# The causal mask of a transformer layer's attention, moved from a matmul in front of the scores to an addition in PSUM behind them

## The chip, the cores and the metric

One NeuronCore of a Trainium2 chip runs the whole kernel; nothing is exchanged with another core. The metric is the device time of one execution in microseconds. The engines that matter here are TensorE (matmuls, written PE in the profile; its weight loads PEld), VectorE (DVE), ScalarE (ACT), GpSimd (POOL) and the DMA queues. Each engine takes its instructions in program order and is kept in step with the others by semaphores.

## What is computed

A pre-norm transformer layer on x of 2 sequences x 1024 positions x 256: attention with 16 heads of 128, then a routed mixture of 32 experts with 8 chosen per token, and two shared blocks.

```python
k = jnp.einsum('ihd,bpd->biph', W_K, x)
q = jnp.einsum('ihd,bpd->biph', W_Q, x)
v = jnp.einsum('ihd,bpd->biph', W_V, x)
scores = jnp.einsum('biph,biqh->biqp', k, q)
mask = jnp.tril(jnp.ones((pos, pos), dtype=x.dtype))
masked = scores * mask - jnp.float32(10000000000.0) * (1.0 - mask)
attn = jax.nn.softmax(masked / jnp.sqrt(jnp.float32(d_head)), axis=-1)
z = jnp.einsum('biqp,biph->biqh', attn, v)
out = jnp.einsum('df,bqf->bqd', W_O, z_flat)
...
x = x + attention(layernorm(x))
x = x + experts(layernorm(x))
```

## The kernel before

**Pairs of heads.** The attention runs over 16 pairs of heads: 8 pairs of sequence 0 (numbered 0 to 7 here), then 8 of sequence 1 (8 to 15). Every product is made as three fp32r matmuls of a high and a low part (`three`, L780 to L784), so each result in PSUM is taken twice: ScalarE copies the high part, VectorE subtracts it from PSUM for the low part.

**Rows of scores.** A head has eight rows of scores, r = 0 to 7; row r is 128 queries by the first 128(r+1) keys. `scores` (L820) writes it into one of two PSUM tiles ps_s of 1024 columns. Its first matmul, L827, is the mask: a bf16 matmul of `causal` (0 on and below the diagonal, -1e30 above) with an identity `ident_bf` into the diagonal 128 columns, with the products then added onto it. VectorE takes the negated maximum of the row (`maximum`, L1310, the reduction at L1312), ScalarE the exponential with the sum of the row (`exponentials`, L1113, at L1116) into `prob`. The tile is free for row r+2 after the exponential.

**What follows a row.** TensorE transposes blocks of prob into one of two banks ps_t (`transpose`, L836, at L841); ScalarE copies the high part pT_hi (L1132) and VectorE makes pT_lo (L1327; pL_hi and pL_lo for the last block of a half); then TensorE multiplies with v into ps_z, VectorE and ScalarE split z (L1334, L1135), and TensorE projects the output into ps_t (two results of 128x256), which VectorE adds to `acc` (L1342). Between these run the projections of the next heads' q, k and v through the bank ps_x, each with its ScalarE copy (L1105, L1107, L1110) and VectorE subtraction (L1298, L1302, L1307).

**The order.** It is written out by hand in tables of items that TensorE, ScalarE and VectorE all walk, each taking its own part of every item. `T` is a transposition, `R` a row of scores, `X` a projection of q, k or v, `V` a product with v, `W` an output projection; the first number is the half (0 to 3: two heads, two halves of 512 queries each). The steady pairs (0 to 6 and 11 to 14, in two loops) use this one:

```python
PAIR = """
T0.0 R0.0 R0.1 T0.1 T0.2 X0 R0.2 R0.3 V0.0 T0.3 X1 V0.1 V0.2 T1.0 T1.1 V0.3 X2 R1.0 R1.1 W0.0
W0.1 X3 V1.0 T1.2 T1.3 R1.2 V1.1 V1.2 V1.3 T1.4 T1.5 X4 V1.4 T1.6 T1.7 R1.3 V1.5 X5 V1.6 V1.7 T2.0
T2.1 R2.0 R2.1 W1.0 X6 T2.2 R2.2 R2.3 W1.1 V2.0 T2.3 X7 V2.1 V2.2 T3.0 T3.1 V2.3 X8 T3.2 R3.0 R3.1
W2.0 X9 W2.1 V3.0 T3.3 V3.1 T3.4 V3.2 T3.5 V3.3 V3.4 T3.6 T3.7 R3.2 V3.5 V3.6 V3.7 X10 R3.3 W3.0 W3.1 X11
"""
```

The rows of a half are made while the half before is worked off: R0.0 to R0.3 are needed whole by T1.0, R1.0 to R1.3 by T2.0, R2.0 to R2.3 by T3.0, R3.0 to R3.3 by the next pair's T0.0. R0.* and R2.* are the wide rows 4 to 7, R1.* and R3.* the rows 0 to 3. Pair 7 (MIDDLE) and pair 8 (ROUTE) have the layer norms and the router's logits woven in, pairs 9 and 10 the routing tables, pair 15 (LAST) has no next pair's rows and ends in the experts. START, in front of pair 0, makes the first four rows and the first projections. Behind the attention (from about 991 us) come the experts, which use ps_s, ps_t and ps_z in other ways.

**Set-up.** GpSimd builds `ident`, `ident_bf`, `causal` and others at the start and counts them on `s_const`; TensorE waits for 8 of them.

Of the kernel before, what the change touches and what calls it, by code (L numbers as in the profile page):

```python
# [12 lines left out]
P = 128  # L13
# [266 lines left out]
def width(r):  # L280

    return P * (r + 1)
# [7 lines left out]
def build(nc, ctx, x, w_a, w_b, w_o, router, bias, experts, out):  # L290
# [12 lines left out]
    xT_lo = sb("xT_lo", [P, ND, B * S], F32R)  # L303
    ident, ident_bf = sb("ident", [P, P]), sb("ident_bf", [P, P], BF16)
    causal = sb("causal", [P, P], BF16)
# [117 lines left out]
    s_pool = sem("pool_hi")  # L423
    s_scores, s_max, s_exp = sem("scores"), sem("max"), sem("exp")
    s_bank, s_hi, s_bank_free = sem("bank"), sem("pT_hi"), sem("bank_free")
# [24 lines left out]
    WS0, YS0 = 16, 16  # L450
    CONSTS = 25 + WORD

# [122 lines left out]
    def _(pool):  # L575
        pool.memset(ident[:, :], 0.0).then_inc(s_const, 1)
        pool.memset(neg_half[:, :], -0.5).then_inc(s_const, 1)
        pool.memset(zero[:, :], 0.0).then_inc(s_const, 1)
        pool.memset(ident_bf[:, :], 0.0).then_inc(s_const, 1)
        pool.memset(causal[:, :], 0.0).then_inc(s_const, 1)  # L580
        pool.wait_ge(s_const, 5)
        for m in (ident, ident_bf):
            pool.affine_select(out=m[:, :], in_=m[:, :], compare_op=ALU.not_equal, fill=1.0,
                               base=0, pattern=[[-1, P]], channel_multiplier=1).then_inc(s_const, 1)
        pool.affine_select(out=causal[:, :], in_=causal[:, :], compare_op=ALU.is_ge, fill=MASKED,
# [60 lines left out]
        pool.iota(thr_int, pattern=[[P, NT]], base=0, channel_multiplier=0).then_inc(s_const, 1)  # L646
        pool.wait_ge(s_const, 18 + 1 + WORD)
        pool.tensor_copy(number[:, :], number_int).then_inc(s_const, 1)
# [127 lines left out]
    def _(pe):  # L776
        pe.sem_inc(s_pv, PV0)
        pe.wait_ge(s_const, 8)

        def three(to, w_hi, w_lo, m_hi, m_lo, start, stop, joins=False):  # L780

            pe.matmul(to, w_hi, m_hi, start=start, stop=False, skip_group_check=joins)  # L782
            pe.matmul(to, w_hi, m_lo, start=False, stop=False, skip_group_check=joins)  # L783
            return pe.matmul(to, w_lo, m_hi, start=False, stop=stop, skip_group_check=joins)  # L784

# [34 lines left out]
        def scores(a, r, row, x_need):  # L820


            pe.wait_ge(s_exp, row + EXP0 - 1)
            pe.wait_ge(s_x_free, x_need + X0)
            q = slice(r * P, (r + 1) * P)
            to = ps_s[r % 2]
            pe.matmul(to[:, r * P:(r + 1) * P], ident_bf[:, :], causal[:, :], start=True, stop=False,  # L827
                      skip_group_check=True)
            for k0 in range(0, width(r), NQ):
                k1 = max(min(width(r), k0 + NQ), k0 + 2 * P)  # L830
                diagonal = k0 <= r * P < k1
                last = three(to[:, k0:k1], q_hi[a][:, q], q_lo[a][:, q], k_hi[a][:, k0:k1],
                             k_lo[a][:, k0:k1], not diagonal, True, diagonal)
            last.then_inc(s_scores, 1)
# [409 lines left out]
    def _(dve):  # L1244
# [65 lines left out]
        def maximum(r, row):  # L1310
            dve.wait_ge(s_scores, row + 1)
            dve.tensor_reduce(neg_max[:, r:r + 1], ps_s[r % 2][:, 0:width(r)], AX.X, ALU.max,  # L1312
                              negate=True).then_inc(s_max, 1)
# [235 lines left out]
        for kind, k, n, m in walk(START):  # L1549
            bank = [ps_x, ps_z][(m or 0) % 2]  # L1550
            if kind == "N":
                norm(k, n)
            elif kind == "Y":
                xn_low(k, n, bank, m)
            elif kind == "X":
                project(k, bank, m)
            elif kind == "R":
                maximum(n, n)
        dve.wait_ge(s_in, 32)
# [105 lines left out]
```

## Time and profile before

| | us |
|---|---|
| time, median of 3 runs | 1381.85 |
| lowest and highest run | 1377.54, 1383.18 |
| profiled execution: its span, first to last instruction | 1405.0 |
| PE busy | 1328.9 (95%) |
| PEld busy | 1171.3 (83%) |
| DVE busy | 905.6 (64%) |
| ACT busy | 722.3 (51%) |
| POOL busy | 571.1 (41%) |

The profiled execution is one execution, 1.7% above the median of the timed ones; no time of it other than its span is given. Rows of the trace are times within it, from its first instruction on. PE's matmuls are pipelined, so their busy times overlap and the distance from one start to the next is what an instruction takes. A bracket at the end of a timeline's row gives the idle time of that engine in front of the row, and the instruction that ended it. Idle time is given only where an engine waited, and a busy sum counts overlap once.

### The profile page before, as it was taken

Reading aid. Unit: us, or ns where it says so; the run is one execution under the profiler, and the core shown is the slowest. Engines: PE = TensorE matmul, PEld = TensorE weight load, DVE = VectorE, ACT = ScalarE, POOL = GpSimd, SP = SyncE. Lnnn points to the kernel's source line nnn. Section 1 sums busy time; section 2 is a strip of 40 time slices with the busy share of each in tenths; the row PEclk is TensorE's granted clock in tenths of the full one; section 3 lists DMA queues with packets and bytes.
Section 4 is the critical chain, followed back from the end, with each engine's and each line's share of the span. In section 5 each row is a group of like instructions: output and inputs, shape, how many; then the busy total and the mean of one; then the engine's idle time right before and its main releaser. Section 6 shows DMA issues by size and latency. Waiting matters only on the chain.

```text
span 1405.0 us, 28535 instructions
## 1 busy us (share of the span) xinstructions
PE 1328.9 (95%) x8578; PEld 1171.3 (83%) x8578; DVE 905.6 (64%) x1875; ACT 722.3 (51%) x1688; POOL 571.1 (41%) x587
## 2 busy tenths in 40 slices
PE   5999999999999899999999999999889997989998
PEld 4888888888888787888778888888779887978886
DVE  5667666666667878687886666666776632345536
ACT  2655555555555555554445555555455553545443
POOL 5535535355232223213043635441003664546554
PEclk9999999999999999999999999999999998999999
DMA  3253544525533000000001201020459996899963
GB/s 118 83 173 105 188 164 133 172 97 183 164 135 102 19 20 16 16 16 20 12 31 60 66 27 68 34 86 0 151 202 311 368 337 237 307 363 378 302 200 116
DMA packets 128246, 195.98 MB, mean 139 GB/s; under 512 B 10400, under 2 KB 99744, under 8 KB 128160
## 3 DMA queue, kind: packets, MB, share of 16 engines
q1 hardware_dynamic: 64752, 110.04, 23.4%
q10 hardware_dynamic: 51120, 51.26, 10.9%
q0 software_dynamic: 12288, 33.57, 6.8%
q8 instruction: 50, 0.82, 0.2%
q14 instruction: 36, 0.29, 0.1%
HBM read 107.79 MB, written 87.03 MB: 139 GB/s over the span
## 4 chain that ended last, share of the span: by engine, by line
PE 82%; DVE 7%; issue 3%; ACT 3%; DMA 3%; another core or an unknown queue 1%; SPq 1%; ACTq 0%; POOL 0%; POOLq 0%; DVEq 0%
PE ps_s L782 9%; PE ps_t L841 8%; PE ps_s L784 8%; PE ps_s L783 8%; PE ps_x L782 6%; PE ps_x L783 6%; PE ps_x L784 6%; PE ps_z L782 5%; PE ps_z L784 5%; PE ps_z L783 5%; PE ps_t L1006 3%; PE ps_z L1006 3%; PE ps_s L975 2%; PE ps_t L782 2%; PE ps_t L783 2%
## 5 line engine op out<-in xcount | busy, mean ns | idle before, releaser
L1116 ACT ACTIVATE prob<-ps_s,neg_max 128x128 f32<-128x128 f32 (+7 forms) x256 | 189.4, 741 | 256.3 <-DVE neg_max L1312 252.1
L1327 DVE TENSOR_TENSOR pT_lo<-ps_t,pT_hi 128x512 fp32r<-128x512 f32 (+2 forms) x320 | 189.4, 603 | 104.9 <-ACT pT_hi L1132 101.3
L1132 ACT ACTIVATE pT_hi<-ps_t 128x512 fp32r<-128x512 f32 (+2 forms) x320 | 161.4, 533 | 94.8 <-PE ps_t L841 92.1
L1312 DVE TENSOR_REDUCE neg_max<-ps_s 128x1 f32<-128x128 f32 (+7 forms) x256 | 186.8, 748 | 14.0 <-PE ps_s L784 11.5
L679 POOL DMA_INDIRECT xs<-xn,slots x128 | 127.7, 997 | 134.8 <-PE ps_z L1006 67.6
L841 PE MATMUL ps_t<-ident,prob 128*128 128x128 f32 x1152 | 170.8, 274 | 9.4 <-ACT prob L1116 4.2
L841 PEld LDWEIGHTS ps_t<-ident,prob 128*128 128x128 f32 x1152 | 136.7, 140 | 33.1 <-DVE pT_lo L1327 5.7
L782 PE MATMUL ps_s<-k_hi,q_hi 128*128 128x512 f32 (+2 forms) x384 | 154.7, 403 | 0.0
L1524 DVE TENSOR_TENSOR h<-sg,ps_s 128x256 f32<-128x256 f32 x112 | 46.9, 418 | 155.9 <-ACT sg L1166 103.9
L782 PE MATMUL ps_s<-ring,a_hi 128*128 x384 | 125.5, 327 | 14.3 <-SPq L530 11.9
L784 PE MATMUL ps_s<-k_hi,q_lo 128*128 128x512 f32 (+2 forms) x384 | 133.7, 348 | 0.0
L783 PE MATMUL ps_s<-k_lo,q_hi 128*128 128x512 f32 (+2 forms) x384 | 132.7, 346 | 0.0
L594 POOL TENSOR_TENSOR a_hi<-raw_a,zero 128x512 fp32r<-128x512 f32 x32 | 33.3, 1041 | 243.3 <-PE ps_x L784 158.3
L782 PE MATMUL ps_z<-pT_hi,v_hi 128*128 128x512 f32 (+2 forms) x320 | 121.8, 381 | 0.5 <-DVE pT_lo L1327 0.5
L784 PE MATMUL ps_z<-pT_hi,v_lo 128*128 128x512 f32 (+2 forms) x320 | 115.5, 361 | 0.0
L783 PE MATMUL ps_z<-pT_lo,v_hi 128*128 128x512 f32 (+2 forms) x320 | 115.4, 361 | 0.0
L1166 ACT ACTIVATE sg<-ps_s 128x256 f32<-128x256 f32 x112 | 43.5, 388 | 139.3 <-PE ps_s L784 82.2
L783 PE MATMUL ps_s<-ring,a_hi 128*128 x384 | 109.9, 286 | 0.1
L784 PE MATMUL ps_s<-ring,a_lo 128*128 x384 | 109.5, 285 | 0.0
L1342 DVE SCALAR_TENSOR_TENSOR acc<-ps_t,inv_sum,acc 128x256 f32<-128x256 f32 x256 | 108.2, 474 | 0.2 <-PE ps_t L784 0.2
L782 PEld LDWEIGHTS ps_s<-ring,a_hi 128*128 128x128 f32 x384 | 74.3, 194 | 24.3 <-issue 22.0
L594 POOL TENSOR_TENSOR o_hi<-raw_o,zero 128x256 fp32r<-128x256 f32 x32 | 20.7, 647 | 168.1 <-PE ps_z L784 167.8
(306 smaller groups left out, 3682.9 us busy)
## 6 DMA issues: line engine op xcount, KB each, us to landing
ring<-ws SPq DMA_DIRECT2D x56, 512.0 KB
xs<-taken SPq DMA_DIRECT2D x16, 1536.0 KB, 9.8
xq<-xs ACTq DMA_DIRECT2D x48, 512.0 KB
xs<-yq ACTq DMA_DIRECT2D x48, 512.0 KB
ws<-split_to SPq DMA_DIRECT2D x34, 512.0 KB, 3.1
raw<-experts_dram SPq DMA_DIRECT2D x34, 256.0 KB, 3.4
raw_a<-w_a_dram SPq DMA_DIRECT2D x15, 512.0 KB, 4.4
ring_down<-experts_dram SPq DMA_DIRECT2D x56, 128.0 KB
```

What stands on the lines that cost most here:

```text
L594: pool.tensor_tensor(hi, src, zero[:, 0:1].to_broadcast([P, src.shape[-1]]), ALU.add).then_inc(s_pool, 1)
L679: pool.indirect_dma_start(xs[b], bass.IndirectOffsetOnAxis(ap=slots[b][:, t, k:k + 1], axis=0), xn[:, t, :], None).then_inc(s_xs[b], 16)
L782: pe.matmul(to, w_hi, m_hi, start=start, stop=False, skip_group_check=joins)
L783: pe.matmul(to, w_hi, m_lo, start=False, stop=False, skip_group_check=joins)
L784: return pe.matmul(to, w_lo, m_hi, start=False, stop=stop, skip_group_check=joins)
L841: last = pe.transpose(bank[:, j * P:(j + 1) * P], prob[c][:, j, n * P:(n + 1) * P], ident[:, :])
L1006: last = pe.matmul(to, hT[g % 2][:, at], downs[g][j], start=what == "m" or j == 0, stop=what == "m" or j == 1)
L1116: act.activation(prob[c][:, j, 0:width(r)], ps_s[r % 2][:, 0:width(r)], ACT.Exp, bias=neg_max[:, r:r + 1], accum_out=row_sum[:, c, j:j + 1 ...
L1132: act.activation(to, ps_t[m % 2][:, j * P:], ACT.Copy).then_inc(s_hi, 1)
L1312: dve.tensor_reduce(neg_max[:, r:r + 1], ps_s[r % 2][:, 0:width(r)], AX.X, ALU.max, negate=True).then_inc(s_max, 1)
L1327: dve.tensor_tensor(lo, ps_t[m % 2][:, j * P:], hi.bitcast(F32), ALU.subtract).then_inc(s_bank_free, 1)
L1342: last = dve.scalar_tensor_tensor(to, ps_t[m % 2][:, j * D:(j + 1) * D], inv_sum[:, c, q:q + 1], to, ALU.mult, ALU.add)
```

## The change

The mask matmul of every row is gone, and with it `ident_bf` and its two set-up instructions on GpSimd. Every group of a row's matmuls now starts afresh. `maximum` first adds `causal` to the diagonal block of the row in PSUM, in place, with a semaphore `s_masked` of its own, and the reduction waits for that. At the first row VectorE also waits for the constants. The tables of items are not touched. The counts of `s_const` are two lower.

```diff
@@ scores, on TensorE
             q = slice(r * P, (r + 1) * P)
             to = ps_s[r % 2]
-            pe.matmul(to[:, r * P:(r + 1) * P], ident_bf[:, :], causal[:, :], start=True, stop=False,
-                      skip_group_check=True)
             for k0 in range(0, width(r), NQ):
                 k1 = max(min(width(r), k0 + NQ), k0 + 2 * P)
-                diagonal = k0 <= r * P < k1
                 last = three(to[:, k0:k1], q_hi[a][:, q], q_lo[a][:, q], k_hi[a][:, k0:k1],
-                             k_lo[a][:, k0:k1], not diagonal, True, diagonal)
+                             k_lo[a][:, k0:k1], True, True)
             last.then_inc(s_scores, 1)
@@ on VectorE
         def maximum(r, row):
             dve.wait_ge(s_scores, row + 1)
+            block = ps_s[r % 2][:, r * P:width(r)]
+            dve.tensor_tensor(block, block, causal[:, :], ALU.add).then_inc(s_masked, 1)
+            dve.wait_ge(s_masked, row + 1)
             dve.tensor_reduce(neg_max[:, r:r + 1], ps_s[r % 2][:, 0:width(r)], AX.X, ALU.max,
                               negate=True).then_inc(s_max, 1)
...
             elif kind == "R":
+                if n == 0:
+                    dve.wait_ge(s_const, MASKS)
                 maximum(n, n)
@@ on GpSimd, set-up
-        pool.memset(ident_bf[:, :], 0.0).then_inc(s_const, 1)
...
-        for m in (ident, ident_bf):
-            pool.affine_select(out=m[:, :], in_=m[:, :], compare_op=ALU.not_equal, fill=1.0,
-                               base=0, pattern=[[-1, P]], channel_multiplier=1).then_inc(s_const, 1)
+        pool.affine_select(out=ident[:, :], in_=ident[:, :], compare_op=ALU.not_equal, fill=1.0,
+                           base=0, pattern=[[-1, P]], channel_multiplier=1).then_inc(s_const, 1)
```

In program order VectorE has, at the head of the steady pair (from the transposition T0.0 to the row R0.3), before:

```order
L1327 TENSOR_TENSOR pT_lo<-ps_t,pT_hi 128x512
L1331 RECIPROCAL inv_sum<-row_sum 128x4
L1311 ISA
L1312 TENSOR_REDUCE neg_max<-ps_s 128x1
L1311 REGISTER_ALU
L1312 TENSOR_REDUCE neg_max<-ps_s 128x1
...
L1302 SCALAR_TENSOR_TENSOR q_lo<-ps_x,q_hi 128x512
L1311 REGISTER_ALU
L1312 TENSOR_REDUCE neg_max<-ps_s 128x1
```

The same place in the changed kernel, from its second subtraction on:

```order
L1326 TENSOR_TENSOR pT_lo<-ps_t,pT_hi 128x384
L1325 REGISTER_ALU
L1326 TENSOR_TENSOR pT_lo<-ps_t,pT_hi 128x256
L1290 ISA
L1298 SCALAR_TENSOR_TENSOR q_lo<-ps_x,q_hi 128x512
L1307 REGISTER_ALU
L1309 TENSOR_TENSOR ps_s<-ps_s,causal 128x128
L1311 TENSOR_REDUCE neg_max<-ps_s 128x1
```

Every reduction has an addition in front of it, and nothing else has moved: in all VectorE's program has 1168 rows where it had 1032.

## Rows read from the trace of the kernel before

**Rows 1.** Windows: us, then each engine's busy us (and instructions), PEclk, DMA share, GB/s
```profile
213.10:272.10 59.00, 59.00 (x379) 52.00 (x378) 39.53 (x76) 32.56 (x76) 27.67 (x24) 1.00 0.46 151
449.00:516.90 67.90, 63.91 (x394) 55.80 (x392) 52.92 (x106) 35.01 (x80) 17.44 (x22) 0.95 0.05 17
516.90:585.20 68.30, 65.31 (x414) 55.55 (x413) 52.47 (x109) 36.02 (x83) 17.45 (x22) 1.00 0.06 17
585.20:648.60 63.40, 60.89 (x381) 52.43 (x380) 49.84 (x132) 32.35 (x77) 13.93 (x12) 1.00 0.06 18
648.60:716.50 67.90, 61.97 (x381) 52.35 (x379) 58.02 (x112) 32.64 (x79) 16.00 (x14) 1.00 0.05 16
776.30:836.10 59.80, 59.36 (x379) 52.08 (x378) 39.59 (x76) 32.34 (x76) 29.28 (x28) 1.00 0.16 53
```

**Rows 2.** Source L827, TensorE: duration ns min/median/max, first and last start
```profile
L827 PE MATMUL ps_s<-causal,ident_bf x256: 216/229/314, 26.2 to 988.4; 128*128 128x128 bf16 x128
```

**Rows 3.** Timeline of TensorE, pair 3, row R0.3: start, us, instruction
```profile
219.19 0.23 PE L827 MATMUL ps_s<-causal,ident_bf 128*128 128x128 bf16 x1
...
219.54 0.39 PE L783 MATMUL ps_s<-k_lo,q_hi 128*128 128x512 f32 x1
219.77 0.39 PE L784 MATMUL ps_s<-k_hi,q_lo 128*128 128x512 f32 x1
```

**Rows 4.** VectorE: two groups by shape (busy, mean ns), then two dependent instructions in order of time
```profile
L1327 DVE TENSOR_TENSOR pT_lo<-ps_t,pT_hi 128x256 fp32r<-128x256 f32 x64 | 26.8, 418 | 16.0 <-ACT pT_hi L1132 14.7
L1327 DVE TENSOR_TENSOR pL_lo<-ps_t,pL_hi 128x128 fp32r<-128x128 f32 x64 | 18.3, 286 | 30.1 <-ACT pL_hi L1132 30.1
...
714.25 0.24 DVE L1499 TENSOR_TENSOR gain<-gain,bit 1x95 f32<-1x95 f32 x1
714.53 0.24 DVE L1501 TENSOR_REDUCE bits<-gain 1x6 f32<-1x96 f32 x1
```

**Rows 5.** Timeline of VectorE, pair 3, head
```profile
215.21 1.85 DVE L1312 TENSOR_REDUCE neg_max<-ps_s 128x1 f32<-128x640 f32 x2
218.49 0.89 DVE L1327 TENSOR_TENSOR pT_lo<-ps_t,pT_hi 128x384 fp32r<-128x384 f32 x2 [1.44 <-ACT pT_hi L1132]
219.30 0.68 DVE L1302 SCALAR_TENSOR_TENSOR q_lo<-ps_x,q_hi 128x512 fp32r<-128x512 f32 x1
219.90 2.22 DVE L1312 TENSOR_REDUCE neg_max<-ps_s 128x1 f32<-128x896 f32 x2
```

**Rows 6.** Timeline of ScalarE, pair 3, head
```profile
217.09 0.90 ACT L1116 ACTIVATE prob<-ps_s,neg_max 128x768 f32<-128x768 f32 x1 [0.17 <-DVE neg_max L1312]
...
221.01 1.01 ACT L1116 ACTIVATE prob<-ps_s,neg_max 128x896 f32<-128x896 f32 x1 [1.79 <-DVE neg_max L1312]
...
222.15 1.12 ACT L1116 ACTIVATE prob<-ps_s,neg_max 128x1024 f32<-128x1024 f32 x1
```

**Rows 7.** Timeline of TensorE, pair 3: the transposes T1.0 and T1.1
```profile
223.78 1.04 PE L841 MATMUL ps_t<-ident,prob 128*128 128x128 f32 x8
```

**Rows 8.** Timeline of ScalarE and TensorE, pair 10: the last wide row and T3.0
```profile
691.95 1.12 ACT L1116 ACTIVATE prob<-ps_s,neg_max 128x1024 f32<-128x1024 f32 x1 [1.17 <-DVE neg_max L1312]
...
693.30 0.96 PE L841 MATMUL ps_t<-ident,prob 128*128 128x128 f32 x7 [0.33 <-ACT prob L1116]
```

**Rows 9.** Timeline of ScalarE and TensorE, pair 3: the last wide row and T3.0
```profile
250.85 1.12 ACT L1116 ACTIVATE prob<-ps_s,neg_max 128x1024 f32<-128x1024 f32 x1 [0.53 <-DVE neg_max L1312]
...
253.19 1.03 PE L841 MATMUL ps_t<-ident,prob 128*128 128x128 f32 x8
```

**Rows 10.** Timeline of VectorE, pair 12: the maximum of row R1.3
```profile
803.35 0.69 DVE L1312 TENSOR_REDUCE neg_max<-ps_s 128x1 f32<-128x512 f32 x1 [1.27 <-PE ps_s L784]
```

**Rows 11.** Timeline, pair 10: TensorE's W0.0, and VectorE without idle time around R2.3
```profile
663.84 0.35 PE L782 MATMUL ps_t<-o_hi,z_hi 128*128 128x256 f32 x1 [0.65 <-DVE pT_lo L1327]
...
690.71 1.22 DVE L1312 TENSOR_REDUCE neg_max<-ps_s 128x1 f32<-128x1024 f32 x1
```

**Rows 12.** Timeline of TensorE, pair 7: the transpose T2.0
```profile
478.31 0.66 PE L841 MATMUL ps_t<-ident,prob 128*128 128x128 f32 x4 [2.13 <-DVE pT_lo L1327]
```

More of the change, by code:

```diff
@@ L303, in build @@
     xT_lo = sb("xT_lo", [P, ND, B * S], F32R)
-    ident, ident_bf = sb("ident", [P, P]), sb("ident_bf", [P, P], BF16)
+    ident = sb("ident", [P, P])
     causal = sb("causal", [P, P], BF16)
@@ L423, in build @@
     s_pool = sem("pool_hi")
-    s_scores, s_max, s_exp = sem("scores"), sem("max"), sem("exp")
+    s_scores, s_masked, s_max, s_exp = sem("scores"), sem("masked"), sem("max"), sem("exp")
     s_bank, s_hi, s_bank_free = sem("bank"), sem("pT_hi"), sem("bank_free")
@@ L450, in build @@
     WS0, YS0 = 16, 16
-    CONSTS = 25 + WORD
+    MASKS = 6
+    CONSTS = 23 + WORD
     X_SCORES = [X0 + x_before + count_of(order, ("M", b, 0)) + 1
@@ L578, in _ @@
         pool.memset(zero[:, :], 0.0).then_inc(s_const, 1)
-        pool.memset(ident_bf[:, :], 0.0).then_inc(s_const, 1)
         pool.memset(causal[:, :], 0.0).then_inc(s_const, 1)
-        pool.wait_ge(s_const, 5)
-        for m in (ident, ident_bf):
-            pool.affine_select(out=m[:, :], in_=m[:, :], compare_op=ALU.not_equal, fill=1.0,
-                               base=0, pattern=[[-1, P]], channel_multiplier=1).then_inc(s_const, 1)
+        pool.wait_ge(s_const, 4)
+        pool.affine_select(out=ident[:, :], in_=ident[:, :], compare_op=ALU.not_equal, fill=1.0,
+                           base=0, pattern=[[-1, P]], channel_multiplier=1).then_inc(s_const, 1)
         pool.affine_select(out=causal[:, :], in_=causal[:, :], compare_op=ALU.is_ge, fill=MASKED,
@@ L646, in _ @@
         pool.iota(thr_int, pattern=[[P, NT]], base=0, channel_multiplier=0).then_inc(s_const, 1)
-        pool.wait_ge(s_const, 18 + 1 + WORD)
+        pool.wait_ge(s_const, 16 + 1 + WORD)
         pool.tensor_copy(number[:, :], number_int).then_inc(s_const, 1)
@@ L777, in _, with three @@
         pe.sem_inc(s_pv, PV0)
[L778 to L784, printed above, removed]
+        pe.wait_ge(s_const, MASKS)
+        def three(to, w_hi, w_lo, m_hi, m_lo, start, stop):
+            pe.matmul(to, w_hi, m_hi, start=start, stop=False)
+            pe.matmul(to, w_hi, m_lo, start=False, stop=False)
+            return pe.matmul(to, w_lo, m_hi, start=False, stop=stop)
         def transpose_xn(q, d, bank):
```

## The prediction

> **What bounds the kernel now.** I read the busy time by stretch first, then TensorE's and VectorE's single rows, then the timeline of one pair of heads on three engines, then the waits. In a steady pair TensorE is busy 59.00 of 59.00 us and VectorE 39.53 [rows 1]. Seven pairs (0 to 6) look like this. So in them every TensorE instruction has its price, and work on VectorE looks free. That second half is what has to be tested, because VectorE and ScalarE take their work in program order and hand each other results. Pairs 7 to 10 carry the layer norm and the routing as well: VectorE is busy 49.84 to 58.02 us of 63.4 to 68.3, and TensorE is idle 2.5 to 5.9 us in each. Pairs 11 to 14 are like pair 12: 59.8 us, TensorE idle 0.4 [rows 1]. Nothing after 991 us touches the change.
>
> **What is removed.** 256 matmuls on TensorE [rows 2]. Their busy 229 ns overlaps others, so the price is taken from starts: from the mask's start to the second ordinary matmul is 219.54 - 219.19 = 0.35 us, and an ordinary one follows the next at 219.77 - 219.54 = 0.23 [rows 3]. A mask costs 0.12 us. 16 a pair make 1.9 us, all 256 make 30.5. The Trainium skill ("TensorE: Matmul & The Clock Gate", section "Back-to-back issue gap") gives about 81 ns to a bf16 matmul of 128 columns in a stream, which would make it 20.7 us. The row decides; what the smaller price would do stands at the sum. The two set-up instructions that GpSimd loses lie in the first 3 us, where TensorE waits for the norm: nothing. Shifting the constants' count moves no wait that ends last.
>
> **What is added.** 256 VectorE additions of 128 columns, PSUM plus SBUF into PSUM, each followed by a wait of the maximum on it. The trace has no write to PSUM by VectorE. The nearest row is the subtraction of 128 columns from PSUM, 286 ns [rows 4]. Today the next instruction starts 0.08 us before its forerunner ends (219.90 against 219.30 + 0.68, [rows 5]); one that waits for its forerunner starts 0.04 us after its end (714.53 against 714.25 + 0.24, [rows 4]). A row of scores then takes VectorE e = 0.286 + 0.04 = 0.32 us more, before its maximum is out. Low end: no overlap is lost, 0.20. High end: the write to PSUM costs as much as 128 columns more, 0.42 [rows 4] + 0.03 = 0.45. I take 0.32, nearest in shape. The Trainium skill ("VectorE: DVE Perf Modes", "The DRAIN you can't avoid") says that a semaphore between two VectorE instructions costs nothing extra, as the next never starts before the pipe is empty. By it e would be 0.29, and the sum 2 us less. These rows disagree by the 0.08.
>
> **Where it falls in a steady pair.** Take the head of pair 3. VectorE reduces two rows from 215.21 on, in 1.85 us, idles 1.44 until ScalarE's copy, takes q_lo at 219.30 and two more rows from 219.90 [rows 5]. ScalarE takes the exponential of the second row at 217.09, having waited for its maximum, then the copies and q_hi, then waits 1.79 for the third row's maximum, and starts the fourth row's exponential at 222.15, which ends at 223.27 [rows 6]. So VectorE's 1.44 of idle time is no cover: it waits there for ScalarE, which waits for VectorE. Step by step: row one is late by 0.32. Row two adds another 0.32, less 0.18 because VectorE waited a little for its scores (an estimate, from the 0.17 that ScalarE idled there): 0.46. The copies, q_hi and q_lo carry 0.46. Rows three and four are back to back: 0.78 and 1.10. TensorE begins the transposes that need row four at 223.78 [rows 7], 0.51 after 223.27. The least distance is seen where it does wait: 693.30 - 693.07 = 0.23 [rows 8]. So 0.28 is slack, and 1.10 - 0.28 = 0.82 us is a new wait on TensorE. The k part of the next projection comes out of the same chain and makes it 0.87. The four masks saved in front of it buy nothing: TensorE only arrives earlier at a later event.
>
> The other twelve masks are worth 12 x 0.12 = 1.43. Against them: the second head chain (rows R2.0 to R2.3) makes its last exponential late by 1.0 us, where TensorE has 253.19 - 251.97 = 1.22 of distance [rows 9], less 0.23 needed and less the masks saved: it gives back 0.14; and the small waits at the output projections and the last products, where a buffer is freed just in time, give back 0.14. Pair: +0.87 - 1.43 + 0.28 = -0.28 us. Seven pairs: **-2.0**.
>
> **Pairs 11 to 14.** VectorE's maximum at 803.35 starts 1.27 us late for no reason that the row shows, [rows 10], and TensorE, whose next transposes need its exponential, is idle 0.44 in the pair [rows 1]. There e adds at once, and what follows on VectorE is late too: I take +0.2 a pair, **+0.8**.
>
> **Pairs 7 to 10.** VectorE is nearly full and TensorE already waits behind it. In pair 10 the waits at 663.84 (0.65) and 693.30 (0.33) stand behind stretches in which VectorE has hardly any idle time (its reduction at 690.71 starts with none in front) [rows 8, 11], so a row of scores in such a stretch costs its 0.32, and the mask saved there nothing. Reading the stretches, I count 11 of 16 rows on the path in pair 10 (+3.6), 7 in pairs 9 and 8 each (+2.3 and +2.1), and 3 in pair 7 after its saved masks (+1.0): **+9.0**. Were all 64 rows on the path it would be +20.5; were none, -7.7.
>
> **Ends.** The last pair's twelve rows partly end in front of the experts: **+1.5**; the four rows of the start: **+0.2**.
>
> **Sum.** -2.0 + 0.8 + 9.0 + 1.5 + 0.2 = +9.5 us: 1414.5 against the profiled 1405.0, which is 1.7% over the median of the runs shown. Carried over to that median, 1381.85 + 9.5 = 1391.4. With e = 0.20 (0.12 less), some 3.7 rows a pair on the chain make seven pairs 3.2 us shorter, pairs 11 to 14 1.0, the 28 rows counted in pairs 7 to 10 3.4 and the ends 0.4: +1.5, 1383. With e = 0.45 (0.13 more) the same steps give 3.4, 2.0, 3.6 and 0.6: +19, 1401. By the 81 ns of the Trainium skill's section, twelve masks a pair would be worth 0.47 less in eleven pairs, and the total 1396.5.
>
> **Rivals.**
> - *TensorE keeps what it is freed of.* If the chain is not serial, that is if the 1.44 us of VectorE idle time does absorb (e below 0.08 would do the same), eleven pairs save 1.9 each: -21, 1361. For it: TensorE 59.00 of 59.00, VectorE a third idle [rows 1]. Against: the releasers in [rows 5, 6], which name each other. 0.12.
> - *The addition is cheap* (e about 0.20): 1383, no change. For it: the maximum's own start overlaps today. Against: its wait on the addition. 0.18.
> - *A dear addition* (e about 0.45): 1401. 0.10.
> - *The stall of pairs 11 to 14 appears in the first loop.* VectorE's program grows by 136 rows; if what holds it at 803.35 depends on where the code lies, seven more pairs cost 59.8 - 59.0 = 0.8 each [rows 1]: +5.6, 1397. If it vanishes instead, -3. 0.10.
> - My forecast, e about 0.32 with the chain as described: 1391. 0.50.
>
> TensorE's clock: in pair 7 the granted clock is 0.95 over the stretch, below full speed after a wait of 2.13 us at 478.31 [rows 1, 12]. That is 0.05 x 67.9 = 3.4 us; another such fall among the new waits is within the range.
>
> **Chances.** What a measurement of this kernel can tell from no change is about 0.5%, 6.9 us. Faster by more: 0.13, the first rival and a little. Within: 0.33, the cheap addition, and the low side of the forecast, since its pairs 7 to 10 rest on a count. Slower by more: 0.54. The 8-in-10 range takes in all but the first rival: 1372 to 1402. It reaches below 1383, because a count of rows on the path that is too high by half would take 4 us off, and the slack of the head chain may be larger than one row shows.
>
> **What would show it.** Right: in the first loop a pair of 58.7 us, no longer full on TensorE, with waits of 0.6 to 1.3 us in front of the transposes that follow the fourth row, released by ScalarE's exponential; additions of about 0.29 us with 0.04 behind them; pair 10 longer by 3 us or more. Wrong: a pair of 57.1 us with TensorE full (the first rival), additions near 0.2 or above 0.4 us, or pairs 7 to 10 unchanged.

## The result and the profile after

The changed kernel takes 1400.45 us, median of 4 runs (1397.79 to 1401.36), beside 1380.59 (1377.54 to 1383.18) for the kernel before. The ratio is 1.0152, with an interval of 1.0129 to 1.0175: 20 us or 1.5% slower. The forecast was 1391.0, that is 9.5 us slower. Sign and range held; the size was half of what came.

| profiled executions, us | before | after |
|---|---|---|
| time of the execution | 1377.02 (a second profile, below) | 1401.36 |
| span | 1375.2 | 1399.6 |
| start of pair 0 | 36.58 | 36.73 |
| pairs 0 to 6, one pair | 58.97 | 59.13 (pair 0: 59.32) |
| pair 7, 8, 9, 10 | 67.79, 68.28, 63.45, 67.86 | 68.81, 72.05, 70.74, 71.51 |
| pairs 11 to 14, one pair | 58.98 | 59.16 |
| pair 15 | 35.08 | 36.86 |
| end of attention | 987.74 | 1007.46 |

A pair's length is the distance from its first TensorE instruction to that of the next pair. The end of attention is taken where the experts' first matmuls begin, behind the last rows of scores; the last products with v still run behind it, among the experts. The first profile of the kernel before was of an execution 1.7% above its median, so the kernel was profiled again (experiment 1), and this table compares with that one. The 20 us lie in attention: +0.15 at the start, +1.3 in pairs 0 to 6, **+15.7 in pairs 7 to 10**, +0.7 in pairs 11 to 14, +1.8 in pair 15, which makes +19.7.

The stretches that answer to [rows 1], in the changed kernel (pair 3, then pairs 7, 8, 9, 10 and 11), columns as there:

```profile
214.32:273.45 59.13, 58.03 (x363) 50.98 (x361) 44.11 (x93) 32.38 (x76) 27.68 (x24) 1.00 0.46 150
...
450.86:519.67 68.81, 62.76 (x378) 54.62 (x377) 57.09 (x123) 34.49 (x80) 17.46 (x22) 0.95 0.06 16
519.67:591.72 72.05, 66.55 (x399) 55.61 (x398) 57.45 (x126) 35.90 (x83) 17.45 (x22) 0.98 0.05 15
591.72:662.46 70.74, 62.70 (x366) 54.12 (x365) 56.54 (x148) 32.67 (x77) 14.04 (x12) 0.95 0.06 16
662.46:733.97 71.51, 61.02 (x365) 51.16 (x363) 62.76 (x128) 32.83 (x79) 16.45 (x14) 1.00 0.05 16
733.97:793.10 59.13, 58.06 (x361) 51.08 (x362) 44.48 (x94) 32.26 (x76) 28.07 (x27) 1.00 0.17 54
```

In pair 3 TensorE is no longer full (58.03 of 59.13), and VectorE has taken on 4.6 us. In pair 9 VectorE's busy time grew by 6.7 us against [rows 1], more than sixteen additions of 0.29 make (4.6), and the granted clock is down to 0.95 where it was 1.00: TensorE was at half speed twice in this pair, from 605.18 and from 656.38 us on, for 3.4 us each. In pair 8 it was once, from 550.57; pair 10, the row that starts at 662.46, has no such fall.

The added instruction, by its source line, and the two largest waits on it and behind it (engine, line, releaser: us in total, times, longest):

```profile
L1309 DVE TENSOR_TENSOR ps_s<-ps_s,causal x256: 272/289/300, 27.5 to 1007.5; 128x128 f32<-128x128 f32 x128
...
ACT prob L1112 <- DVE neg_max L1311: 322.9, 255, 4.9
...
PE ps_t L837 <- ACT prob L1112: 25.5, 19, 3.6
```

289 ns, against 286 of the nearest row in [rows 4]: writing to PSUM costs VectorE next to nothing. TensorE's transposes now wait 25.5 us for ScalarE's exponential, in 19 places; in the second profile of before it was 2.5 us in 4.

The head of pair 3 in the changed kernel: VectorE, then TensorE's T1.0, which answers to [rows 5, 7]:

```profile
221.57 0.29 DVE L1309 TENSOR_TENSOR ps_s<-ps_s,causal 128x128 f32<-128x128 f32 x1
221.89 1.09 DVE L1311 TENSOR_REDUCE neg_max<-ps_s 128x1 f32<-128x896 f32 x1
222.90 0.29 DVE L1309 TENSOR_TENSOR ps_s<-ps_s,causal 128x128 f32<-128x128 f32 x1
223.22 1.23 DVE L1311 TENSOR_REDUCE neg_max<-ps_s 128x1 f32<-128x1024 f32 x1
...
225.74 1.15 PE L837 MATMUL ps_t<-ident,prob 128*128 128x128 f32 x8 [1.10 <-ACT prob L1112]
```

From an addition's start to its maximum's start is 0.32 us (221.57 to 221.89), as forecast. T1.0 waits 1.10 us for the exponential, at the place that was named and within the 0.6 to 1.3 that was named. So in the steady pairs the mechanism is the forecast one. The question for the experiments is where the other 10 us come from.

### The profile page after: what moved, and what is told of

The parts are those of the page before. It is cut to its first block, busy times and chain, and to the rows that moved or that the text cites. A ratio compares the mean times of both kernels' runs of the same rounds, so it can differ in the third digit from the quotient of the medians.

```text
span 1399.6 us, 28277 instructions
## 1 busy us (share of the span) xinstructions
PE 1306.7 (93%) x8322; PEld 1158.2 (83%) x8322; DVE 984.8 (70%) x2131; ACT 731.6 (52%) x1688; POOL 570.0 (41%) x585
## 4 chain that ended last, share of the span: by engine, by line
PE 66%; DVE 18%; issue 6%; DMA 5%; ACT 4%; SPq 0%; ACTq 0%; POOL 0%; POOLq 0%; DVEq 0%
PE ps_t L837 7%; PE ps_s L781 6%; PE ps_s L783 6%; PE ps_s L782 6%; PE ps_x L781 5%; DVE neg_max L1311 5%; PE ps_x L782 5%; PE ps_x L783 5%; DMA ring_down<-experts_dram 4%; PE ps_z L781 4%; PE ps_z L783 4%; PE ps_z L782 4%; PE ps_t L1002 3%; PE ps_z L1002 3%; DVE pT_lo L1326 3%
## 5 line engine op out<-in xcount | busy, mean ns | idle before, releaser
L837 PE MATMUL ps_t<-ident,prob 128*128 128x128 f32 x1152 | 175.2, 277 | 34.8 <-ACT prob L1112 25.5
L1311 DVE TENSOR_REDUCE neg_max<-ps_s 128x1 f32<-128x128 f32 (+7 forms) x256 | 194.0, 758 | 8.7
L781 PE MATMUL ps_s<-k_hi,q_hi 128*128 128x512 f32 (+2 forms) x384 | 144.0, 375 | 2.0 <-DVE k_lo L1303 1.5
```

What stands on the lines that cost most here:

```text
L781: pe.matmul(to, w_hi, m_hi, start=start, stop=False)
L837: last = pe.transpose(bank[:, j * P:(j + 1) * P], prob[c][:, j, n * P:(n + 1) * P], ident[:, :])
```

## The experiments

The time of before beside them was 1376.9 to 1377.9 us. In the hybrid kernels below a function `by_dve(name, k, n)` says which rows Rk.n VectorE masks; for the others the mask matmul stays. `name` is the order that the row stands in: START, PAIR (pairs 0 to 6 and 11 to 14), MIDDLE, ROUTE, SLOTS, DISPATCH (pairs 7, 8, 9, 10) and LAST (pair 15).

**1. The kernel before again** (no edit).

> The kernel before once more, for a profile taken beside its timed runs (the first profile was of an execution 1.7% longer than the median). Theory A (the 20 us arise inside attention): attention ends at 989 to 992 us again, the steady pair is 58.96 us, pairs 7 to 10 take 267 to 268 us together, and what follows attention takes about 392 us, as in the profile of the changed kernel. Theory B (part of the 20 us lies behind attention): what follows attention takes under 390 us. The one stall of VectorE of about 1.27 us in each of pairs 11 to 14 is expected again (59.75 us a pair).

Measured: 1377.82 us, ratio 1.0008 (0.9992 to 1.0024). Attention ends at 987.74, the steady pair is 58.97, pairs 7 to 10 take 267.4, what follows attention takes 387.5, against 392.1 in the profile of the changed kernel. 387.5 is under the 390 of theory B; but what follows attention took 387.6 to 393.0 us in the later profiles (391.2 in experiment 9, which is faster than before, 388.1 in experiment 10 with the same code there), so 5 us there are scatter, and the 19.7 us inside attention match the timed 19.9 by themselves. The stall of 1.27 us of [rows 10] is gone: pairs 11 to 14 take 58.96 to 59.02 us.

```profile
716.77:775.80 59.03, 59.03 (x377) 52.05 (x378) 40.06 (x78) 32.45 (x76) 28.39 (x27) 1.00 0.17 55
```

TensorE is full in pair 11. That stall belonged to one execution, not to the kernel.

**2. No mask at all.**

```diff
-            pe.matmul(to[:, r * P:(r + 1) * P], ident_bf[:, :], causal[:, :], start=True, stop=False,
-                      skip_group_check=True)
```

> Leaves the causal mask out altogether: no mask matmul, no addition. What TensorE's side of the change is worth by itself. Theory A (a mask matmul costs 0.12 us of TensorE wherever TensorE sets the pace): a steady pair takes 57.3 us (16 rows, 12 to 16 of them at 0.12), pairs 7 to 10 lose 4 to 5 us together, whole kernel 20 to 25 us less than before (about 1357), no fall of the clock in pairs 8 to 10. Theory B (a back-to-back matmul of 128 columns costs 0.08): a steady pair of 57.7 us, whole kernel about 15 us less.

Measured: 1358.51 us, ratio 0.987 (0.9853 to 0.9887), 18 us less. A steady pair takes 57.37 us (theory A), pairs 7 to 10 lose 3.1 together, less than theory A's 4 to 5, and the total lies between the theories. Sixteen masks give back 1.60 us, 0.10 each. That lies between the 0.12 taken and the 0.08 of the Trainium skill ("TensorE: Matmul & The Clock Gate", "Back-to-back issue gap").

**3. Mask matmul and addition.**

```diff
+                dve.tensor_tensor(block, block, causal[:, :], ALU.add).then_inc(s_masked, 1)
+                dve.wait_ge(s_masked, masked)
```

> Keeps the mask matmul and makes VectorE's addition too (the mask is added twice): VectorE's side by itself. Theory A (the two sides add up): a steady pair of 59.18 + what the kernel without any mask saves a pair, so 60.6 to 60.9 us; pairs 7 to 10 take 16 + 4 = 20 us more than before; whole kernel 38 to 45 us above before. It shows falls of the clock in pairs 8 to 10 as the changed kernel does. Theory B (the additions overlap with the matmuls and the changed kernel's 20 us are mostly clock falls and waits that the missing matmuls bring): whole kernel about 20 to 28 us above before.

Measured: 1409.85 us, ratio 1.0243 (1.0222 to 1.0264), 33 us above before. A steady pair takes 60.03, 1.06 above before. Pairs 7 to 10 take 282.4, **15.0 above before, with all the mask matmuls in place**; without them, in the changed kernel, 283.1. So in pairs 7 to 10 the freed matmuls are worth next to nothing beside the additions, which cost it all. The clock blurs this a little: this kernel had no fall in pair 8, one in pair 9 and one in pair 10. With the prices that are worked out below the freed matmuls come to about 1 us, an estimate. Both theories miss the total: the sides don't add up. Without any mask the additions cost a steady pair 59.13 - 57.37 = 1.76, beside the masks 1.06, since in a head TensorE, freed of its masks, only arrives earlier at the same wait.

**4. Only the rows outside PAIR on VectorE.**

```diff
+def by_dve(name, k, n):
+    return name != "PAIR"
```

> VectorE masks only the rows outside the repeated order PAIR: the head, pairs 7 to 10 and pair 15 (80 of 256 rows); the matmul masks the others. Theory A (the loss arises in pairs 7 to 10): steady pairs 58.96 us, pairs 7 to 10 together 283 us as in the changed kernel (before 267.5), whole kernel 17 to 20 us above before; three falls of the clock, one in each of pairs 8, 9 and 10. Theory B (the clock falls come of TensorE's doing less in all pairs): no such falls, and pairs 7 to 10 take 278 us, whole kernel 11 to 13 us above before.

Measured: 1396.27 us, ratio 1.0144 (1.0126 to 1.0161), 19 us. Steady pairs 58.97, pairs 7 to 10 282.8, pair 15 36.84. Theory A holds for the times: 80 of 256 rows make nearly the whole loss. It missed on the clock, which fell in pairs 7 (as in before), 8 and 9 and not in pair 10. The expected fall in pair 10 seems to be the changed kernel's at 656.38 us, but that one lies in pair 9, which ends at 662.46. Pair 10 has no fall in either kernel and takes 71.48 here and 71.51 there, so its 3.7 us are the additions' alone. Where pair 10 did have a fall, in experiments 3 and 11, it came 48 to 50 us into the pair, and from T3.1 to T3.2 TensorE's delay grew by 1.2 us; in the changed kernel it grew by nothing there. (The delay of an instruction is its start, counted from its pair's first transposition, less the same in the second profile of before.)

**A look into pair 9.** Pair 9 alone had grown by 7.3 us, and half of it appears at one instruction, T1.0, at which the delay grows by 3.7 us, against 1.2 to 1.6 in the other pairs. VectorE, then GpSimd in the same stretch, in the changed kernel:

```profile
598.97 2.44 DVE L1366 TENSOR_TENSOR biased<-score,bias_bc 128x256 f32<-128x256 f32 x1
...
598.74 2.39 POOL L596 TENSOR_TENSOR v_lo<-v_raw,v_hi 128x1024 fp32r<-128x1024 f32 x1
```

and in the kernel before (second profile):

```profile
592.22 0.44 DVE L1367 TENSOR_TENSOR biased<-score,bias_bc 128x256 f32<-128x256 f32 x1
...
592.46 2.46 POOL L597 TENSOR_TENSOR v_lo<-v_raw,v_hi 128x1024 fp32r<-128x1024 f32 x1
```

The same addition takes 2.44 us instead of 0.44. Before, it had started 0.24 us ahead of GpSimd's v_lo. Now the additions of R0.0 and R0.1 bring it 0.23 us behind, and it ends when v_lo does (601.41 and 601.13). The Trainium skill ("GPSIMD Engine Reference", "Specifications") says that GpSimd shares its SBUF interfaces with VectorE, with contention when a VectorE instruction has two SBUF inputs: score and bias_bc are two. That section gives no size; here it is the whole rest of the other engine's instruction, 2.0 us. Behind it TensorE waits 3.57 us, and then runs slowly:

```profile
605.60 1.94 PE L837 MATMUL ps_t<-ident,prob 128*128 128x128 f32 x8 [3.57 <-ACT prob L1112]
...
607.98 0.63 PE L781 MATMUL ps_x<-xT_hi,b_hi 128*128 128x512 f32 x1
608.40 0.48 PE L782 MATMUL ps_x<-xT_lo,b_hi 128*128 128x512 f32 x1
608.73 0.39 PE L783 MATMUL ps_x<-xT_hi,b_lo 128*128 128x512 f32 x1
608.96 0.40 PE L781 MATMUL ps_x<-xT_hi,b_hi 128*128 128x512 f32 x1
```

A matmul of 512 columns is followed by the next after 0.42 us at 607.98 and after 0.23 at 608.73: TensorE ran at 1.2 GHz, from 605.18 us on, within its long wait, and is back at 2.4.

**5. That addition moved behind R0.3.** Only VectorE's order of pair 9 changes.

```diff
+SLOTS.remove(("G", 0, 0))
+SLOTS.insert(SLOTS.index(("R", 0, 3)) + 1, ("G", 0, 0))
```

> The changed kernel with one VectorE item of pair 9 (G0.0, the addition that writes biased) placed behind row R0.3 instead of ahead of R0.2. In the changed kernel this addition took 2.44 us instead of 0.44, from 598.97 to 601.41, and it ended as GpSimd's v_lo<-v_raw,v_hi did, which had begun 0.2 us before it. Theory A (the two engines exclude each other there, so the addition waits out GpSimd's 2.4 us): behind R0.3 it takes 0.4 us, the first transpose T1.0 of pair 9 comes 2.4 us earlier (2.0 collision, 0.4 its own place), pair 9 takes 68.1 to 68.7 us instead of 70.74, the whole kernel is 2 to 3 us faster than the changed one (ratio to before about 1.013). Theory B (the 2 us are an instruction load or the like, bound to the instruction): it keeps 2.4 us in its new place, and pair 9 gains at most 0.4 us.

```profile
602.57 0.41 DVE L1368 TENSOR_TENSOR biased<-score,bias_bc 128x256 f32<-128x256 f32 x1
...
599.55 2.39 POOL L598 TENSOR_TENSOR v_lo<-v_raw,v_hi 128x1024 fp32r<-128x1024 f32 x1
...
604.04 1.06 PE L839 MATMUL ps_t<-ident,prob 128*128 128x128 f32 x8 [1.20 <-ACT prob L1114]
```

The addition is at 0.41 us, TensorE's wait at 1.20. Theory A, and more than it said: pair 9 takes 66.44 us, 4.3 less instead of the 2.1 to 2.6 expected. The whole kernel takes 1396.91 us, ratio 1.0136 (1.0121 to 1.0152), 3.5 less than the changed kernel's median. T1.0's delay is 0.77 us instead of 3.14: 2.4 of the 4.3 are the collision (2.0) and the instruction's own place (0.4). The other 1.9 are two falls of the clock that are gone. The one behind the long wait is worth 0.4 of them: from T1.0 to T1.1 the changed kernel's delay grows by 0.41, here by nothing, and at T2.0 the kernels are still 2.8 apart. Granted clock (the last but two number of a row) in the changed kernel behind its wait, then here:

```profile
604.00:608.00 4.00, 2.40 (x12) 2.43 (x13) 2.30 (x9) 2.88 (x6) 0.00 (x0) 0.65 0.09 29
608.00:612.00 4.00, 4.00 (x26) 3.69 (x26) 3.26 (x9) 1.63 (x4) 0.00 (x0) 0.93 0.00 0
```

```profile
604.00:608.00 4.00, 3.67 (x23) 3.14 (x23) 3.64 (x11) 2.73 (x6) 0.00 (x0) 1.00 0.11 33
```

The other 1.5 are the fall from 656.38 to 659.79, at the end of pair 9. TensorE's wait ahead of it and the granted clock, in the changed kernel:

```profile
655.85 0.39 PE L781 MATMUL ps_x<-a_hi,xT_hi 128*128 128x256 f32 x1 [1.49 <-DVE room L1590]
...
655.00:659.00 4.00, 3.15 (x14) 2.97 (x15) 1.11 (x2) 1.43 (x5) 0.00 (x0) 0.67 0.01 4
659.00:663.00 4.00, 4.00 (x31) 3.89 (x30) 2.98 (x7) 1.18 (x5) 0.23 (x1) 0.90 0.00 0
```

From the last transposition, T3.7, to the end of the pair the delay grows from 5.57 to 7.30 us; here from 2.81 to 2.99, without a fall, though TensorE waits the same 1.49 us at the same instruction. Experiment 4 has no fall there either, behind 1.48 us, and experiment 12 has one, behind 1.48. So this fall does not follow from the moved addition, and no run shows what decides whether it comes.

**6. The same move in the kernel before**, the control.

> The same move in the kernel before, where the addition had begun 0.24 us ahead of GpSimd's v_lo and took 0.44 us: the control. Theory A: pair 9 gains at most its own 0.4 us (63.1 to 63.5 us), whole kernel the same within 0.1%. Theory B: the same.

Measured: ratio 1.0002 (0.9992 to 1.0012), pair 9 at 63.10 us, 0.35 less, as both theories said. In its new place the addition starts 1.91 us behind a v_lo of 2.40 us and takes 0.78: it meets the last 0.5 us of it. With the 2.22 us that it takes in experiment 12, where it starts 0.46 behind v_lo, and the 2.44 and 2.45 of experiments 4 and 3, 0.23 behind, the delay shrinks with what is left of GpSimd's instruction. In experiment 11 the addition starts 0.05 us ahead and takes 0.42, and v_lo takes 2.62 instead of 2.39.

**7. Outside PAIR, all rows but R0.\* on VectorE.**

```diff
+def by_dve(name, k, n):
+    return name not in ("PAIR", "START") and k != 0
```

> Outside PAIR and START, VectorE masks all rows but R0.0 to R0.3 (those ahead of a pair's first transposes T1.0); the matmul masks these and all rows of the steady pairs. 48 + 8 = 56 rows of 256 are on VectorE. Theory A (half of the loss arises at T1.0, which waits for the exp of R0.3): pairs 7 to 10 take 267.4 + 7 to 9 us together, pair 9 about 66 us, the addition that writes biased is at 0.44 us again, pair 15 about 35.8 us; whole kernel 8 to 10 us above before. Theory B (every addition weighs alike): three quarters of the loss stay, pairs 7 to 10 at 267.4 + 11 to 12 us, whole kernel 13 to 14 us above before.

Measured: 1387.64 us, ratio 1.0068 (1.0051 to 1.0085), 9 to 10 us. Pairs 7 to 10 take 67.21, 71.03, 65.67 and 70.32, together 6.8 above before; pair 15 takes 35.83, and the addition that writes biased is short again. Theory A, just below its 7 to 9 us for these pairs: the sixteen rows R0.\* of these four pairs, a quarter of them, carried 15.4 - 6.8 = 8.6 of the 15.4 us of experiment 4, collision and slow stretch of pair 9 included.

**8. Only R0.\* of the steady pairs on VectorE** (`name == "PAIR" and k == 0`).

> VectorE masks only R0.0 to R0.3 of the steady pairs (44 rows of 256); the matmul masks all others. Theory A (the steady pair's +0.17 us is the sum of two opposite parts: the chain ahead of T1.0, and what the other twelve masks give back, which the kernel not_heads showed as -0.74): a steady pair of 58.97 + 0.17 + 0.74 = 59.88 us (59.8 to 60.0), TensorE waits 1.1 us ahead of T1.0, whole kernel 9 to 11 us slower than before. Theory B (the costs of the rows mix and don't add): a steady pair of 59.1 to 59.6 us, whole kernel 2 to 6 us slower.

```profile
217.16:277.16 60.00, 58.90 (x374) 51.91 (x373) 40.64 (x80) 32.56 (x76) 27.67 (x24) 1.00 0.45 148
```

Measured: 1389.56 us, ratio 1.0078 (1.0059 to 1.0097). A steady pair takes 60.00 us, with TensorE 1.10 short of full, all in front of T1.0. Theory A.

**9. All but R0.\* of the steady pairs on VectorE** (`name == "PAIR" and k != 0`).

> VectorE masks the rows R1.* to R3.* of the steady pairs (11 pairs of 12 rows, 132 of 256); the matmul masks R0.* there and everything outside them. Theory A (the only addition chain that TensorE feels in a steady pair is that of R0.0 to R0.3, which costs it 1.26 us at T1.0; the other twelve are free, and each gives back 0.08 to 0.12 us): a steady pair of 57.7 to 58.1 us (58.97 less twelve times 0.08 to 0.12, plus up to 0.3 at T3.0), the rest as before, whole kernel 10 to 13 us faster than before (ratio 0.991 to 0.993), faster than both kernels. Theory B (the additions delay the later transposes too, T3.0 and T3.4 first): a steady pair of 58.6 to 59.0 us, whole kernel within 4 us of before.

```profile
211.34:269.58 58.24, 58.24 (x367) 51.09 (x366) 43.00 (x89) 32.38 (x76) 27.69 (x24) 1.00 0.46 152
```

Measured: 1369.29 us, ratio 0.9940 (0.9926 to 0.9954), **8 us faster than before** and 31 faster than the changed kernel. A steady pair takes 58.24 us with TensorE full: theory A's side, though short of its 57.7 to 58.1 and of its 10 to 13 us. Twelve rows give back 0.74 (8 and 9 together: +1.03 - 0.74 = +0.29, where the changed kernel shows +0.16).

**10. The same, with R1.\* to R3.\* of pair 7 and R3.\* of pair 8.**

> not_heads, and in addition VectorE masks R1.* to R3.* of pair 7 and R3.* of pair 8, where the kernel late_rows showed TensorE ahead of before (pair 7: 67.21 us against 67.79; in pair 8 0.08 us from each row of R3). Theory A: pair 7 at 66.7 to 67.2 us, pair 8 at 67.9 to 68.3, whole kernel 8 to 10 us faster than before, 0.5 to 1 us faster than not_heads, which the timing cannot resolve but the pairs' lengths can. Theory B (the gain of pair 7 in late_rows came from its shorter fall of the clock, 3.4 us instead of 6.8, and not from the masks): pair 7 anywhere from 67.2 to 67.8, no gain over not_heads.

Measured: 1368.83 us, ratio 0.9930 (0.9912 to 0.9948). Pair 7 at 67.32, pair 8 at 68.17. In experiment 9 pair 7 took 67.23 without one VectorE mask in it, and its clock was at half speed for 3.4 us instead of 6.8 as in before. So theory B is right for pair 7; beyond experiment 9 there is nothing to be had here that a timing shows.

**11. The sum written aside.** The maximum reads the unmasked scores and waits for no addition.

```diff
-            dve.tensor_tensor(block, block, causal[:, :], ALU.add).then_inc(s_masked, 1)
-            dve.wait_ge(s_masked, row + 1)
+            dve.wait_ge(s_masked, row)
+            dve.tensor_tensor(masked[:, :], block, causal[:, :], ALU.add).then_inc(s_masked, 1)
```

> The changed kernel with the addition's result written to a tile of its own in SBUF, so that the maximum reads the unmasked scores and needn't wait for the addition; this leaves the causal mask out of the result. It measures what the dependence of the maximum on the addition costs beyond the addition's own 0.288 us. Theory A (0.04 us a row, and an addition costs 0.29 us in any place): a steady pair of 58.9 to 59.05 us (four rows at 0.04 less), whole kernel 2 to 4 us faster than the changed one. Theory B (the dependence costs nothing that matters, as by the Trainium skill's page on VectorE, where every VectorE instruction ends with a drain): a steady pair within 0.05 us of 59.13, whole kernel within 1.5 us. Theory C (a result in SBUF instead of PSUM makes the addition itself shorter): additions under 0.25 us, whole kernel over 5 us faster.

Measured: 1378.16 us, ratio 0.9995 (0.9985 to 1.0006). With all 256 additions still there, 279 ns each, it is **22 us faster than the changed kernel**, five times what theory A said. A steady pair takes 58.17, pairs 7 to 10 take 273.4. VectorE in the head of pair 3:

```profile
218.31 0.28 DVE L1310 TENSOR_TENSOR masked<-ps_s,causal 128x128 f32<-128x128 f32 x1
218.50 1.08 DVE L1311 TENSOR_REDUCE neg_max<-ps_s 128x1 f32<-128x896 f32 x1
219.50 0.28 DVE L1310 TENSOR_TENSOR masked<-ps_s,causal 128x128 f32<-128x128 f32 x1
219.70 1.21 DVE L1311 TENSOR_REDUCE neg_max<-ps_s 128x1 f32<-128x1024 f32 x1
```

Start to start is 0.19 to 0.20 us now, with the wait 0.32. All three theories counted from an addition's end (0.04 us behind it). But an instruction that waits for nothing starts 0.08 to 0.09 *before* the end of the one ahead, so the wait costs 0.13 a row. In a steady pair that makes 0.96 us at more than one place. T1.0 waits 0.55 us instead of 1.10, which is the four rows R0.\*. From T3.0 to T3.2, the first that need the rows R2.\*, the changed kernel falls behind before by another 0.31 (no idle time is shown there, but the starts are further apart), and this one by nothing. The last 0.1 comes at the end of the pair. In pairs 7 to 10 it is 9.7 us, of which 5.7 in pair 9, but not all of that is the wait: the collision (2.4 us) and the changed kernel's falls of the clock in pairs 8 and 9 (1.4 and 1.9) are absent here, and pair 10 has a fall that costs 1.2. That leaves about 5 us for the rows. The place of the result is changed together with the wait here; the next experiments keep it in PSUM.

**12 to 14. Two additions, then two maxima.** Where two rows stand next to each other in the order, both additions come first; result in PSUM and wait as in the changed kernel. In all pairs, then in the steady pairs alone, then for the rows of experiment 9 and those of pair 7.

```diff
+                if not follows:
+                    add_mask(r, row)
+                if ahead:
+                    add_mask(r + 1, row + 1)
                 dve.wait_ge(s_masked, masked)
```

> The changed kernel with the additions of two adjacent rows of the order (R0.0 and R0.1, R0.2 and R0.3, and so on) issued one after the other ahead of the first row's maximum; addition, maximum and wait are the same, in PSUM, only another instruction stands between an addition and the maximum that waits for it. aside changed both the wait and the place of the result. Theory A (what aside won is the wait for the instruction just ahead: start to start 0.32 us with it, 0.19 without, so 0.13 a row): a pair of additions and the wait costs 0.38 us instead of 0.64, T1.0 comes 0.4 to 0.55 us earlier, a steady pair 58.3 to 58.7 us instead of 59.13, pairs 7 to 10 some 5 to 9 us less than the changed kernel's 283 together, whole kernel 10 to 17 us faster than the changed one, from 4 us faster to 8 us slower than... before's 1377.5 taken as 0: +3 to +10 us. Theory B (it was the result in SBUF instead of PSUM): no gain, a steady pair at 59.0 to 59.2, whole kernel within 2 us of the changed one.

> The same for the rows of the steady pairs alone; in all other pairs the mask matmul is back. It parts the steady pairs' share of paired_all from that of pairs 7 to 10. Theory A: a steady pair as in paired_all (58.3 to 58.7 us), pairs 7 to 10 as before (267.4), whole kernel 3 to 8 us faster than before. Theory B: a steady pair at 59.0 to 59.2 and the whole kernel 0 to 3 us slower than before.

> VectorE masks R1.* to R3.* of the steady pairs and of pair 7, with adjacent rows' additions together; the matmul masks R0.* and everything else. Theory A (in not_heads T3.0 still waited for the chain of R2.0 to R2.3, worth some 0.2 to 0.3 us): a steady pair of 57.9 to 58.15 us instead of 58.23, whole kernel 9.5 to 13 us faster than before, faster than best. Theory B (T3.0 isn't held by VectorE's chain): a steady pair of 58.2 to 58.3 us, the same as not_heads within 1.5 us.

Measured: all pairs 1397.10 us, ratio 1.0140 (1.0124 to 1.0156), a steady pair at 59.20; steady pairs alone 1381.41, ratio 1.0028 (1.0017 to 1.0039), 59.20; the last 1372.22, ratio 0.9963 (0.9949 to 0.9977), 58.36. All three are nearer to theory B, though outside its bounds: the first is 3.4 us faster than the changed kernel (bound 2), the second 3.5 slower than before (3), the third 2.9 slower than experiment 9 (1.5), with a pair of 58.36 (58.3). The rows say something else. VectorE in the head of pair 3, all pairs:

```profile
217.25 0.27 DVE L1346 TENSOR_TENSOR ps_s<-ps_s,causal 128x128 f32<-128x128 f32 x1
217.92 0.30 DVE L1346 TENSOR_TENSOR ps_s<-ps_s,causal 128x128 f32<-128x128 f32 x1 [0.39 <-PE ps_s L816]
218.12 1.68 DVE L1357 TENSOR_REDUCE neg_max<-ps_s 128x1 f32<-128x640 f32 x2
...
222.65 0.49 DVE L1346 TENSOR_TENSOR ps_s<-ps_s,causal 128x128 f32<-128x128 f32 x2
223.04 2.21 DVE L1357 TENSOR_REDUCE neg_max<-ps_s 128x1 f32<-128x896 f32 x2
```

For R0.2 and R0.3 two additions and their waits take 0.39 us (222.65 to 223.04) instead of 0.64: the price of the wait is indeed hidden by another instruction in between, with the result in PSUM, and TensorE waits 0.68 us at T1.0 instead of 1.10. But for R0.0 and R0.1 VectorE stands 0.39 us in front of the second addition, because TensorE has not finished R0.1's scores, and R0.0's maximum stands behind it. That takes back what the other pair wins (59.19 against 59.13 in pair 3). The same happens in pairs where R0 isn't masked, hence 58.36 instead of 58.24. Pairing only where both rows' scores are there was not tried.

One row of evidence fell out of it. In pair 8 of experiment 12 the clock did not fall. From T1.6 to V1.6 TensorE's delay against before stays as it is, where in the changed kernel, at half speed in that stretch, it grows from 1.98 to 3.40 us. Experiment 3, which has no fall there either, is a closer comparison: its delay is 2.00 at T1.6 and 1.99 at T2.0, against 1.98 and 3.43 in the changed kernel. So the fall in pair 8 costs about 1.4 us.

## Why the prediction was half right

**"In a steady pair VectorE's second half looks free, and is not": right.** TensorE's wait stands in front of T1.0, 1.10 us long, released by ScalarE's exponential; a pair is no longer full on TensorE. The rival by which TensorE keeps its time would have shown 57.1 us.

**"e = 0.286 + 0.04 = 0.32": right,** 0.289 and 0.03, start to start 0.32. Right too was to keep the rule on the drain at a distance. By the Trainium skill ("VectorE: DVE Perf Modes", "The DRAIN you can't avoid") a semaphore between two VectorE instructions costs nothing extra; experiment 11 shows 0.13 us a row. The same section of the Trainium skill adds that a next instruction that is not held back starts earlier. Experiment 11 agrees with that: the maximum starts 0.08 to 0.09 us before the end of the addition. Wrong was the weight of e: the low end, 0.12 less, was reckoned at 8 us less, and 0.13 less measured 22, of which some 4.5 are the collision and the clock. In eleven steady pairs it is 10.6 (0.96 each, where 3.7 rows on the chain made 0.45): the head's four rows give 0.55 of that, and the rest lies at T3.0 to T3.2 and the pair's end, which the forecast counted at almost nothing. In pairs 7 to 10 it is 9.7, about 5 without collision and clock (forecast 3.4).

**"Pair: +0.87 - 1.43 + 0.28 = -0.28 us": off by 0.44,** measured +0.16 (the first pair +0.34). The head costs 1.03 instead of 0.87 (experiment 8), the other twelve give back 0.74 instead of 1.15 (experiment 9): a mask is worth 0.10, not 0.12, and the small waits give back 0.46, not 0.28, of which 0.31 lie from T3.0 to T3.2, where the second head chain was reckoned at 0.14. Over seven pairs -2.0 became +1.3: **3.3 us of the miss.**

**"Pairs 11 to 14: +0.8": +0.7 measured, by luck.** The stall on which it rested was not there in the second profile of before, nor in any later one. The rival that gave it to the first loop rested on the same row.

**"Pairs 7 to 10: I count 28 rows, +9.0": the step that failed,** at +15.7, 6.7 us of the miss. By pair, forecast and measured: pair 7 +1.0 and +1.0, pair 10 +3.6 and +3.7, pair 8 +2.1 and +3.8, pair 9 +2.3 and +7.3. The match in pair 7 is in part luck, since with the code of before that pair took 67.23 to 68.10 us in six profiles, by the place and length of its fall of the clock. The count of rows was nearly right. Two things that a count of rows can't hold came on top: VectorE's collision with GpSimd in pair 9 (2.4, experiment 5), and the clock at half speed: two falls in pair 9 (0.4 and 1.5, experiment 5) and one in pair 8 (about 1.4, experiments 3 and 12). Pair 10 had none. 15.7 - 2.4 - 3.3 leaves 10.0 for the rows. The text had put "another such fall" of the clock into the range, and no part of it into the sum, where three came; the collision it did not see, though both instructions stand in the trace of before, 0.24 us apart.

**"Ends: +1.5 and +0.2":** +1.8 and +0.15.

## What to carry to other kernels

When work moves to an engine that is a third idle, look at where its results are waited for, row by row: here four of sixteen rows of a pair cost TensorE 1.03 us and the other twelve gain 0.74, so a split by row beats both whole versions by 8 and 31 us. Price an added dependent instruction from start to start, and count what the wait takes away from overlap. Where a step delays an engine, look for what it will newly meet there: an instruction of another engine that had just been missed by 0.2 us can cost more than the step itself. Where TensorE newly waits its clock may fall as well; a fall of 3.4 us cost 0.4 to 1.5 here. Behind the same wait it came in some profiles and not in others, so look up when it began in each before a difference is put down to the edit.

## What the runs showed of the hardware

- A VectorE addition of 128 columns into PSUM, in place, takes 289 ns, about as one that writes to SBUF does (286 for the subtraction, 279 in experiment 11).
- Two VectorE instructions without a wait between them overlap by 0.08 to 0.09 us. A wait for the instruction just ahead makes 0.32 us start to start out of 0.19; with one more instruction in between the wait costs nothing (0.39 us for two).
- A VectorE addition with two SBUF inputs, started 0.23 us behind a GpSimd instruction of 2.39 us, took 2.44 us instead of 0.44; started 0.46 us behind, 2.22; started 1.91 us behind, 0.78. Started 0.24 us ahead of it, it was not slowed.
- Around a TensorE wait of 3.57 us the clock went to its lower level for 3.4 us, which cost 0.4; with that wait at 1.20 us in the same place it stayed at 2.4 GHz. Falls of the same length cost 1.4 in pair 8, 1.5 at the end of pair 9 and 1.2 in pair 10.
- Behind a wait of 1.48 to 1.49 us at the end of pair 9 the clock fell in two kernels (changed, experiment 12) and stayed up in two (experiments 4 and 5).
- A VectorE stall of 1.27 us in each of four pairs was there in one execution of the kernel before, and in neither of the two later profiles of that code.
